# A three-layer graph convolution: the last 148 nodes as an eleventh pair of the seven-product scheme, and all combined operands of the W2 product kept in SBUF

## Chip, cores, metric

One core of one Trainium2 chip. The metric is the device time of one launch in microseconds, median of the runs.

## What is computed

```python
def _gc(x, adj, W, b):
    return adj @ (x @ W) + b
h = jnp.maximum(_layernorm(x, axis=-1), 0.0)
h1 = relu(_gc(h, adj, W1, b1));  h2 = relu(_gc(h1, adj, W2, b2))
out = x + _gc(h2, adj, W3, b3)
```

x is 2708 x 512, adj 2708 x 2708 (dense fp32), W1 512 x 1024, W2 1024 x 1024, W3 1024 x 512. The kernel works on transposed operands (`adjT`, `xT`), with nodes split in two column halves of 1354 (`HALF`), each stored with a stride of 1360.

## The kernel before

**Arithmetic.** Every fp32 operand is cut in two: ScalarE casts it to the matmul's reduced format ("hi"), VectorE subtracts that from the operand ("lo"), and TensorE makes three products (`three`: hi x hi, hi x lo, lo x hi) into one PSUM bank.

**Stages.** Pass 1: adj x LN(x), times 512 features, result `P1` in DRAM. h1 phase: `P1` times W1, in 22 blocks of nodes. Pass 2: adj x h1 for 1024 features. w2 phase: times W2. w3 phase: h2 times W3, again in 22 blocks. Pass 3: adj x (h2 W3), plus b3 and x. Passes and the w2 phase run over three column chunks of 512, 512 and 330 nodes per half (`WIDTH`).

**Seven products.** Pass 2, the w2 phase and pass 3 use a Strassen-like scheme with seven products per chunk: parts `X11, X12, S2, S3, S1, X22, S4` = 0 to 6. A product contracts over ten pairs of 128-node blocks (t, t+10). `DIRECT` parts take raw blocks of adj, the others read combinations that GpSimd made (`TS` in DRAM). Each (chunk, part) is a group on 4 banks in pass 2 and in the w2 phase, on 2 banks in pass 3. Nodes 2560 to 2707 are outside the pairs: block 20 (128 nodes, `left`) with three matmuls per bank, and the 20-node tail (`SHORT`), whose three products are stacked in the rows of one matmul (three loads of 20 rows at `STEP` = 32). They are not in the scheme, so they are added once for every output quarter: in the groups of parts 1, 5 and 6 and in one more with part `None`, which in pass 2 runs inside the group behind (`inner`, `INNER`). `left_over` issues these matmuls (L1811 to L1825).

**Order.** `plan_main` writes one list of steps, which all engines walk in the same order: "cut" (load a raw tile, SyncE; cast, ScalarE; subtract, VectorE), "tail", "drain", "stat", "combine", "store". Raw tiles go through five raw buffers (`RAW`), cut moving tiles through a ring of five (`RING`). `later` places a drain some cuts behind its group. Tiles of h1 or W2 for a later part (`s`, `w2s`) are put between the moving tiles (`spread_in`).

**w2 phase.** Chunk 0's combined operands are made by GpSimd (`prep_moving`, L1618) from `P2` and stored in DRAM (`T2`), from where SyncE loads them (L1023) as raw tiles. For chunks 1 and 2 GpSimd makes them in SBUF (`hold`, `prep_held`, L1641), and they need no raw buffer. Drains of part 0 go to the buffers e(0..3) by ScalarE (L1226), those of the other running sum to e(4..7); finished quarters are stored from these buffers and from `spill` (L1251).

**Start.** `statistics`, `root`, `centre` and `inverse` make the layer norm of each x tile: VectorE and ScalarE take turns.

The change touches `plan_main`, the loads of SyncE, the cuts and drains of ScalarE and VectorE, GpSimd's preparation, and TensorE's group functions.

Of the kernel before, what the change touches and what calls it, by code (L numbers as in the profile page):

```python
# [19 lines left out]
SHORT = 21  # L20
ORDER = (1, 2, 3, 4, 5, 6, 0, 7, 8, 9)
EARLY = 8
BLOCKS = [b for t in ORDER for b in (t, t + PAIRS)] + [20, SHORT]
# [17 lines left out]
HOLD = {S2: 0, S3: 1, S1: 2, X22: 3}  # L41
# [11 lines left out]
INNER = 5  # L53


class Tile:


    def __init__(self, kind, cut):
        self.kind, self.cut = kind, cut  # L60
        self.raw = self.raw_freed = self.slot = None

        self.loads = self.raw_count = None
        self.block = self.part = self.pair = self.chunk = self.half = self.k = None

        self.freed = self.place_freed = None


class Group:


    def __init__(self, phase, chunk, part, banks):
# [3 lines left out]
        self.inner = None  # L76
# [6 lines left out]
class Plan:  # L83
    def __init__(self):
        self.steps, self.groups = [], []
        self.cuts = self.raws = self.slots = self.tails = 0
# [19 lines left out]
    def tile(self, kind, ring, loads=1):  # L106

        j = Tile(kind, self.cuts)
        self.cuts += 1
        if loads:  # L110
            self.take_raw(j, loads)
# [9 lines left out]
    def take_raw(self, j, loads):  # L121
        j.raw = self.raws
        before = self.raw_user[j.raw % RAW]
        j.raw_freed = before.cut + 1 if before else None
# [49 lines left out]

def columns_chunk(block):
    first = block * P
    last = min(first + P, 2 * HALF) - 1
    return max(sum(c % HALF >= a for a in START) - 1 for c in range(first, last + 1))
# [14 lines left out]
def plan_pass1():  # L193
# [31 lines left out]
    for c in range(CHUNKS):  # L225
        mine = []
        for n, b in enumerate(BLOCKS[:-1]):
# [50 lines left out]
def plan_main():  # L278
# [9 lines left out]
    def tail_step(g, c, half):  # L288
        p.tails += 1
        g.tail = (p.tails, c, half, at["tail_freed"][p.tails % 2])  # L290
# [3 lines left out]
    def h1_phase(lag):  # L294
        def emit(g, j):
            def go():
# [3 lines left out]
                if b == SHORT:  # L300
                    p.steps.append(("short", (g, p.drained)))
                    p.later(5, lambda: p.steps.append(("short_stat", (g,))))
                    return
# [4 lines left out]
                if b == 20:  # L308
                    p.stationary("h1", 20, 0, turn, side)
# [8 lines left out]
        for j, b in enumerate(BLOCKS):  # L318
            g = p.group("h1", None, None, [(2 * j) % 8, (2 * j + 1) % 8])
            g.block = b  # L320
            t = p.tile("h1", True, 3 if b == SHORT else 1)
# [4 lines left out]
            p.later(lag if b != SHORT else LAG, emit(g, j))  # L326


    def pass2():
# [10 lines left out]
        leftover = None  # L340
        for part in range(7):
            if part == 0:
                extra = []
            elif part < 6:
                extra = [lambda t=t, i=part + 1: load_h1(i, t) for t in ORDER]
            else:
                extra = [lambda q=q, i=i: load_w2(i, q) for i in (X11, X12, S2) for q in range(4)]
            half = {1: 0, 5: 0, 6: 1}.get(part)
            for c in range(CHUNKS):
# [3 lines left out]
                if leftover:  # L353
                    g.inner = p.group("pass2", leftover.chunk, None, leftover.banks)
                    leftover = None
                for i, t in enumerate(ORDER):
# [3 lines left out]
                    p.release(j, g, half is None and i == PAIRS - 1)  # L360
                    last_of[part, t] = j.freed
                    p.emit_due()
                    if g.inner and i == 0:
                        tail_step(g.inner, g.inner.chunk, 1)
                    if g.inner and i == INNER - 1:
                        k = p.tile("left", True)
                        k.chunk, k.half = g.inner.chunk, 1
                        g.inner.left = k
                        p.release(k, g.inner, True)
                        at["tail_freed"][g.inner.tail[0] % 2] = g.inner.done[-1]  # L370
                        p.later(LAG, lambda q=g.inner: drain2(q))
                        p.emit_due()
                    if half is not None and i == (8 if g.inner else 6):
                        tail_step(g, c, half)
# [3 lines left out]
                if half is not None:  # L378
                    k = p.tile("left", True)
                    k.chunk, k.half = c, half  # L380
                    g.left = k
                    p.release(k, g, True)
                    at["tail_freed"][g.tail[0] % 2] = g.done[-1]
                    p.emit_due()
                last_of["end", part] = g.done[-1]
                p.later(LAG, lambda g=g: drain2(g))
                if part == 4:
                    leftover = g
# [3 lines left out]
    def drain2(g):  # L392
# [3 lines left out]
        if part in (1, 4):  # L396
# [3 lines left out]
            at["staged", c] = bufs  # L400
        elif part is None:
            bufs = at["staged", c]
# [8 lines left out]
        if bufs and part != 4:  # L411
# [9 lines left out]
    def w2_phase():  # L421
# [9 lines left out]
        for c in range(CHUNKS):  # L431
            for part in range(7):
# [6 lines left out]
                if c == 2 and part > 2:  # L439
                    extra = [lambda k=k: load_w3(k) for k in (2 * part - 6, 2 * part - 5)]  # L440
                for q in range(4):
                    held = c > 0 and part in HOLD
# [12 lines left out]
    def drain_w2(g, ms):  # L455
        part = g.part
        spare = [("g", m if g.chunk == 0 else m % 2) for m in ms]
        p.count_drains(g, ms, 2 if part == 4 else 1)
        finals = {1: [("e", 4 + m) for m in ms], 4: spare, 5: [("e", 4 + m) for m in ms],
                  6: [("e", m) for m in ms]}.get(part)  # L460
        needs = {0: [("e", m) for m in ms], 1: [("e", 4 + m) for m in ms], 3: [("e", 4 + m) for m in ms],
# [21 lines left out]
    def w3_phase(lag):  # L483
# [18 lines left out]
        def emit(g, j):  # L502
            def go():
                b = g.block
                if b == SHORT:
                    p.drained += 1
                    g.free_drained = p.drained
                    p.steps.append(("short", (g, p.drained)))
                    p.later(5, lambda: p.steps.append(("short_stat", (g,))))
                    first = late[:2]  # L510
                    del late[:2]
                    for f in first:
                        f()
# [1425 lines left out]
```

## Time and profile before

| | |
|---|---|
| median of three runs | 1592.84 us (1591.72 to 1594.43) |
| the profiled execution | 1593.0 us, span 1591.2 us |
| TensorE matmuls | 7674, busy 1581.1 us (99%) |
| VectorE, ScalarE, GpSimd busy | 872.1, 610.6, 456.3 us |
| DMA | 303.37 MB, mean 191 GB/s |

"Busy" of TensorE is the union of its matmuls, whose ends are modelled and overlap the next one's start. A row of the timeline gives start, length, engine, line, operation, output <- inputs, shapes, and in brackets the idle time before it with what ended it.

### The profile page before, as it was taken

How to read it: one execution, taken by the hardware profiler on the slowest of the kernel's cores; microseconds unless marked ns; L12 is line 12 of the kernel's file. 1: busy time of each engine (PE TensorE's matmuls, PEld its weight loads, DVE VectorE, ACT ScalarE, POOL GpSimd, SP SyncE). 2: the span in 40 equal slices, each digit the busy share in tenths (PEclk: the TensorE clock that was granted, in tenths of full speed). 3: DMA queues.
4: the chain of work that ended last, by engine and by line, in shares of the span. 5: the costliest groups of instructions: out<-in, count | busy, mean ns of one | idle time of the engine just before them, and what ended most of it. 6: DMA issues, size and time to landing. Idle time of an engine off the chain costs nothing.

```text
span 1591.2 us, 20930 instructions
## 1 busy us (share of the span) xinstructions
PE 1581.1 (99%) x7674; PEld 1360.1 (85%) x7674; DVE 872.1 (55%) x1361; ACT 610.6 (38%) x1076; POOL 456.3 (29%) x417
## 2 busy tenths in 40 slices
PE   9999999999999999999999999999999999999999
PEld 7788889988889898989898989788898888888898
DVE  8973433256553443434564446564565538766856
ACT  5442222234433332323332333443455536454444
POOL 5863544336654000000000015345402214201302
PEclk9999999999999999999999999999999999999999
DMA  6975657644567554545455658884645336887866
GB/s 244 321 225 205 222 179 220 204 138 152 176 220 235 151 153 143 142 118 148 143 169 161 175 186 282 275 298 133 206 120 133 93 93 202 251 249 220 252 191 198
DMA packets 196628, 303.37 MB, mean 191 GB/s; under 512 B 22632, under 2 KB 92608, under 8 KB 196524
## 3 DMA queue, kind: packets, MB, share of 16 engines
q1 hardware_dynamic: 162268, 223.12, 47.1%
q0 software_dynamic: 12224, 43.16, 8.4%
q10 hardware_dynamic: 22032, 35.74, 6.3%
q8 instruction: 61, 1.00, 0.3%
q14 instruction: 43, 0.35, 0.1%
HBM read 219.44 MB, written 82.50 MB: 190 GB/s over the span
## 4 chain that ended last, share of the span: by engine, by line
PE 91%; DVE 5%; DMA 3%; ACT 1%; issue 0%; ACTq 0%; DVEq 0%
PE ps L1731 30%; PE ps L1733 30%; PE ps L1732 30%; DVE slots L1350 1%; PE ps L1824 1%; DVE still L1332 1%; DMA H<-parts 1%; DVE stats L1279 1%; DMA raw<-adjT 0%; DMA raw<-W 0%; DVE ring L1360 0%; DMA raw<-TS 0%; DMA P<-stage_b 0%; DMA raw<-T 0%; ACT slots L1099 0%
## 5 line engine op out<-in xcount | busy, mean ns | idle before, releaser
L1360 DVE TENSOR_TENSOR ring<-raw,ring 128x512 fp32r<-128x512 f32 (+1 forms) x562 | 404.7, 732 | 426.6 <-ACT ring L1131 424.1
L1131 ACT CAST ring<-raw 128x512 fp32r<-128x512 f32 (+1 forms) x562 | 321.3, 577 | 561.9 <-PE ps L1733 464.8
L1731 PE MATMUL ps<-slots,still 128*128 128x512 f32 (+1 forms) x504 | 183.6, 364 | 2.3 <-DVE slots L1350 1.4
L1733 PE MATMUL ps<-slots,still 128*128 128x512 f32 (+1 forms) x504 | 183.1, 363 | 0.0
L1732 PE MATMUL ps<-slots,still 128*128 128x512 f32 (+1 forms) x504 | 183.1, 363 | 0.0
L1733 PE MATMUL ps<-ring,even 128*128 128x512 f32 (+1 forms) x480 | 174.6, 364 | 0.0
L1732 PE MATMUL ps<-ring,even 128*128 128x512 f32 (+1 forms) x480 | 174.6, 364 | 0.0
L1731 PE MATMUL ps<-ring,even 128*128 128x512 f32 (+1 forms) x480 | 174.6, 364 | 0.0
L1587 POOL DMA_DIRECT2D prep<-P x40 | 26.4, 662 | 465.2 <-DMA P<-U 434.4
L1731 PE MATMUL ps<-ring,S 128*128 128x512 f32 (+1 forms) x420 | 153.0, 364 | 0.6 <-DVE ring L1360 0.6
L1733 PE MATMUL ps<-ring,S 128*128 128x512 f32 (+1 forms) x420 | 152.5, 363 | 0.0
L1732 PE MATMUL ps<-ring,S 128*128 128x512 f32 (+1 forms) x420 | 152.5, 363 | 0.0
L1350 DVE TENSOR_TENSOR slots<-raw,slots 128x1024 fp32r<-128x1024 f32 (+2 forms) x64 | 86.3, 1348 | 118.5 <-ACT slots L1099 118.4
L1733 PE MATMUL ps<-ring,odd 128*128 128x512 f32 (+1 forms) x360 | 131.1, 364 | 0.0
L1732 PE MATMUL ps<-ring,odd 128*128 128x512 f32 (+1 forms) x360 | 131.1, 364 | 0.0
L1731 PE MATMUL ps<-ring,odd 128*128 128x512 f32 (+1 forms) x360 | 131.0, 364 | 0.0
L1731 PE MATMUL ps<-ring,W2c 128*128 128x512 f32 (+1 forms) x336 | 122.8, 365 | 2.6 <-ACT parts L1226 1.5
L1732 PE MATMUL ps<-ring,W2c 128*128 128x512 f32 (+1 forms) x336 | 122.5, 365 | 0.0
L1733 PE MATMUL ps<-ring,W2c 128*128 128x512 f32 (+1 forms) x336 | 122.5, 365 | 0.0
L1099 ACT CAST slots<-raw 128x1024 fp32r<-128x1024 f32 (+2 forms) x64 | 59.7, 933 | 142.8 <-PE ps L1733 134.2
L1731 PEld LDWEIGHTS ps<-slots,still 128*128 128x128 f32 x504 | 94.8, 188 | 18.3 <-DVE slots L1350 3.8
L1733 PEld LDWEIGHTS ps<-slots,still 128*128 128x128 f32 x504 | 94.8, 188 | 13.2
(162 smaller groups left out, 2891.1 us busy)
## 6 DMA issues: line engine op xcount, KB each, us to landing
raw<-TS SPq DMA_DIRECT2D x160, 256.0 KB, 2.9
raw<-adjT SPq DMA_DIRECT2D x138, 256.0 KB, 3.1
raw<-adjT SPq DMA_DIRECT2D x41, 512.0 KB, 4.6
TS<-made SPq DMA_DIRECT2D x20, 1024.0 KB, 6.6
raw<-TS SPq DMA_DIRECT2D x80, 165.0 KB, 2.4
raw<-HS SPq DMA_DIRECT2D x50, 256.0 KB, 2.7
raw<-P SPq DMA_DIRECT2D x45, 256.0 KB, 4.0
raw<-adjT SPq DMA_DIRECT2D x68, 165.0 KB, 2.6
```

What stands on the lines that cost most here:

```text
L1099: act.copy(slot1(j, 0, a, j.chunk), raw1[:, j.raw % RAW1, a, 0:w]) \
L1131: act.copy(hi, src).then_inc(hi_done, 1)
L1279: dve.bn_stats(stats[rows, half:half + 6], tile).then_inc(stats_done, 1)
L1332: dve.scalar_tensor_tensor(still[:, j.block, 1, :], xin[:, j.block, 1, :], x_column(n, "scale"), still[:, j.block, 0, :].bitcast(F32), ALU ...
L1350: dve.tensor_tensor(slot1(j, 1, a, j.chunk), raw1[:, j.raw % RAW1, a, 0:w], slot1(j, 0, a, j.chunk).bitcast(F32), ALU.subtract).then_inc(l ...
L1360: dve.tensor_tensor(lo, src, hi.bitcast(F32), ALU.subtract).then_inc(lo_done, 1)
L1587: pool.dma_start(dst, src).then_inc(prep_in[i], 16)
L1731: pe.matmul(out, st_hi, mv_hi, start=start, stop=False)
L1732: pe.matmul(out, st_hi, mv_lo, start=False, stop=False)
L1733: return pe.matmul(out, st_lo, mv_hi, start=False, stop=stop)
L1824: pe.matmul(ps[:, g.banks[m], 0:w], tail[0:REP, cols], slot_tails[g.tail[0] % 2][0:REP, 0:w], start=False, stop=True).then_inc(group_done, 1)
```

## The change

The 148 last nodes become an eleventh pair (`EXTRA`) of two blocks of 74 nodes (`REST`), with all seven products. So every group of pass 2 and pass 3 (21 each) ends with `extra_pair`: per bank two matmuls over 128 rows that hold the three stacked products: rows 0 to 73 of the first lo x hi, rows 74 to 127 of it and 74 to 127 of the second hi x hi, rows 0 to 73 of the second hi x lo. `AGAIN` (54) rows and the other `ONCE` (20) are loaded a second time for that. The part `None` and `inner` are gone. The stationary combinations of the extra pair go through DRAM (`HX`, `HX3`) and come back as tiles `extra2` (two per part) and `extra3` (one per group of pass 3, four transfers); the combined rows of adj come from `TX`, which GpSimd makes after the h1 phase. In the w2 phase `hold` serves chunk 0 as well: S2, S3 are made beside pass 2, S1, X22 once pass 2 is over and U is stored; the places in `HOLD` are reversed, and `T2` is gone. `sides` swaps e(0..3) and e(4..7) from chunk to chunk. The blocks of the h1 and w3 phases run with the extra pair in the ninth place. At the start, `root(1)`, `centre(1)` and `inverse(1)` move behind the cut of the first tile's second half. In pass 3 the part-4 group finishes three quarters (before: two in part `None`, one in part 4).

```diff
+REST = 74
+EXTRA = PAIRS
+BLOCKS = [b for t in ORDER[:EARLY] + (EXTRA,) + ORDER[EARLY:] for b in ((20, 21) if t == EXTRA else (t, t + PAIRS))]
+AGAIN = P - REST
+ONCE = REST - AGAIN
-HOLD = {S2: 0, S3: 1, S1: 2, X22: 3}
+HOLD = {S2: 3, S3: 2, S1: 1, X22: 0}
...
+def sides(chunk):
+    return (0, 4) if chunk % 2 == 0 else (4, 0)
...
+        def load_extra(part):
+            first = p.tile("extra2", False, 2)
+            second = p.tile("extra2", False, 2, low=False)
+            for row, j in enumerate((first, second)):
+                j.part, j.half = part, row
+                j.place_freed = ("group", last_of["end", part - 2]) if part > 1 else None
...
-                extra = []
+                extra = [lambda i=i: load_extra(i) for i in (X11, X12)]
             elif part < 6:
-                extra = [lambda t=t, i=part + 1: load_h1(i, t) for t in ORDER]
+                extra = [lambda i=part + 1: load_extra(i)] + [lambda t=t, i=part + 1: load_h1(i, t) for t in ORDER]
...
-                    if n % 3 == 1 if part < 6 else n > 3 and n % 2 == 0:
+                    if n % 5 in (1, 3) if part < 6 else n > 3 and n % 2 == 0:
                         spread_in(extra)
...
-                    held = c > 0 and part in HOLD
+                    held = part in HOLD
...
-            for part in (0, 1, 2, 3, None, 4, 5, 6):
+            for part in range(7):
...
+                    if i == 2:
+                        k = p.tile("extra3", False, 4)
+                        n = 7 * c + part
+                        k.part, k.pair = part, n % 3
+                        k.place_freed = ("group", ends[n - 3] if n > 2 else w3_end)
...
-    left = place("left", [P, 2, H], F32R, left_at)
+    extra_at += -extra_at % BANK
+    extra2 = place("extra2", [P, 2, 2, F], F32R, extra_at)
...
                 elif j.kind == "left":
-                    sp.dma_start(raw[:, r, 0:WIDTH[j.chunk]], adjT[20 * P:21 * P, columns(j.half, j.chunk)]) \
-                        .then_inc(raw_in[r], 16)
+                    w = WIDTH[j.chunk]
+                    sp.dma_start(raw[0:REST, r, 0:w], extra_rows(j.part, j.chunk, 0, REST)).then_inc(raw_in[r], 16)
+                    sp.dma_start(raw[REST:P, r, 0:w], extra_rows(j.part, j.chunk, 0, AGAIN)).then_inc(raw_in[r], 16)
+                elif j.kind == "extra2":
...
+                    sp.dma_start(raw[0:REST, r, :], src).then_inc(raw_in[r], 16)
+                    sp.dma_start(raw[REST:P, r, :], src[again, :]).then_inc(raw_in[r], 16)
+                elif j.kind == "extra3":
...
+                    for half in range(2):
+                        cols = slice(half * QUARTER, (half + 1) * QUARTER)
+                        again = slice(0, AGAIN) if half == 0 else slice(ONCE, REST)
+                        sp.dma_start(raw[0:REST, r, cols], src).then_inc(raw_in[r], 16)
+                        sp.dma_start(raw[REST:P, r, cols], src[again, :]).then_inc(raw_in[r], 16)
...
-                    for r in range(3):
-                        sp.dma_start(raw_tail[r * STEP:r * STEP + TAIL, 0, 0:WIDTH[c]],
-                                     adjT[SHORT * P:N, columns(half, c)]).then_inc(tail_in, 16)
+                    sp.dma_start(raw_tail[0:REST, 0, 0:w], extra_rows(a.part, c, 0, REST)).then_inc(tail_in, 16)
+                    sp.dma_start(raw_tail[REST + AGAIN - ONCE:P, 0, 0:w], extra_rows(a.part, c, AGAIN, REST)) \
+                        .then_inc(tail_in, 16)
...
                 for second in (False, True):
+                    if second and c == 0:
+                        pool.wait_ge(group_done, at["pass2_end"])
+                        for u in range(CHUNKS):
+                            pool.wait_ge(u_stored[u], 16 * KF)
...
+            def extra_pair(g, ms, first, second):
...
+                    pe.matmul(out, first[:, cols], ring[:, j.slot % RING, 0, 0:w], start=False, stop=False)
+                    pe.matmul(out, second[:, cols], slot_tails[g.tail[0] % 2][:, 0:w], start=False, stop=True) \
+                        .then_inc(group_done, 1)
```

## Rows read from the trace of the kernel before

**Rows 1.** The page: span, TensorE's busy time, its granted clock in 40 slices.
```profile
span 1591.2 us, 20930 instructions
...
PE 1581.1 (99%) x7674; PEld 1360.1 (85%) x7674; DVE 872.1 (55%) x1361; ACT 610.6 (38%) x1076; POOL 456.3 (29%) x417
...
PEclk9999999999999999999999999999999999999999
```

**Rows 2.** Stages: us, busy (x count) of PE, PEld, DVE, ACT, POOL, clock, DMA share, GB/s.
```profile
0.00:76.00 76.00, 72.80 (x299) 56.63 (x300) 69.69 (x155) 38.52 (x66) 51.03 (x35) 1.00 0.80 277
...
439.00:987.00 548.00, 548.00 (x2713) 476.50 (x2712) 255.13 (x395) 170.88 (x309) 59.73 (x70) 1.00 0.57 173
987.00:1141.00 154.00, 152.89 (x675) 126.17 (x674) 92.20 (x131) 65.18 (x108) 68.37 (x72) 1.00 0.69 225
...
1314.00:1519.00 205.00, 205.00 (x907) 169.80 (x906) 149.24 (x205) 103.40 (x179) 48.23 (x42) 1.00 0.78 233
1519.00:1591.00 72.00, 68.48 (x451) 67.37 (x449) 46.95 (x92) 33.95 (x76) 11.39 (x14) 1.00 0.70 201
```

**Rows 3.** Timeline of TensorE in pass 2, first matmul of and behind two blocks.
```profile
538.78 0.40 PE L1731 MATMUL ps<-ring,left 128*128 128x512 f32 x1
...
542.51 0.39 PE L1731 MATMUL ps<-ring,odd 128*128 128x512 f32 x1
...
591.87 0.32 PE L1731 MATMUL ps<-ring,left 128*128 128x330 f32 x1
...
594.34 0.40 PE L1731 MATMUL ps<-ring,even 128*128 128x512 f32 x1
```

**Rows 4.** The same in pass 3, one wide block.
```profile
1340.94 0.39 PE L1731 MATMUL ps<-ring,left 128*128 128x512 f32 x1
...
1342.76 0.39 PE L1731 MATMUL ps<-ring,S 128*128 128x512 f32 x1
```

**Rows 5.** Timeline of TensorE: four stands, at the start, in w2, in pass 3.
```profile
10.94 0.50 PE L1731 MATMUL ps<-slots,still 128*128 128x512 f32 x1 [0.89 <-DVE slots L1350]
...
1032.12 0.50 PE L1731 MATMUL ps<-ring,W2c 128*128 128x512 f32 x1 [1.11 <-DVE ring L1360]
...
1157.17 0.39 PE L1731 MATMUL ps<-ring,W2c 128*128 128x330 f32 x1 [1.52 <-ACT parts L1226]
...
1550.27 0.42 PE L1731 MATMUL ps<-ring,S 128*128 128x330 f32 x1 [0.56 <-DVE ring L1360]
```

**Rows 6.** Timeline of ScalarE before the stand at 1032.
```profile
1028.52 0.62 ACT L1131 CAST W2c<-raw 128x512 fp32r<-128x512 f32 x1 [2.32 <-DMA raw<-W]
```

**Rows 7.** Timeline of VectorE, cut of the first tile's second half.
```profile
10.19 0.69 DVE L1350 TENSOR_TENSOR slots<-raw,slots 128x512 fp32r<-128x512 f32 x1 [0.21 <-ACT slots L1099]
```

**Rows 8.** Timeline of ScalarE's and GpSimd's queues: U stores, and loads that begin steps.
```profile
997.06 1.35 ACTq L1243 DMA_DIRECT2D P<-U  x3
...
1020.03 1.29 POOL L1587 DMA_DIRECT2D prep<-P  x2 [10.97 <-DMA H<-parts]
...
1031.71 1.28 POOL L1587 DMA_DIRECT2D prep<-P  x2 [0.30 <-POOL hold L1670]
...
1060.64 0.72 POOL L1587 DMA_DIRECT2D prep<-P  x1 [0.30 <-POOL hold L1670]
...
1068.98 1.28 POOL L1587 DMA_DIRECT2D prep<-P  x2 [0.31 <-POOL hold L1664]
```

**Rows 9.** Timeline of ScalarE at the end of the h1 phase: relu, then casts.
```profile
434.66 1.06 ACT L1175 ACTIVATE pair_buf<-pair_buf 128x1024 f32<-128x1024 f32 x1 [2.84 <-DVE pair_buf L1402]
...
436.71 1.65 ACT L1131 CAST ring<-raw 128x512 fp32r<-128x512 f32 x3
```

**Rows 10.** The DMA view: packets; issues with KB each and median us to landing.
```profile
DMA packets 196628, 303.37 MB, mean 191 GB/s; under 512 B 22632, under 2 KB 92608, under 8 KB 196524
...
P<-U ACTq DMA_DIRECT2D x4, 165.0 KB, 4.5
...
raw_tail<-adjT SPq DMA_DIRECT2D x48, 40.0 KB
```

More of the change, by code:

```diff
@@ L104, in later, with tile @@
         self.pending.sort(key=lambda q: q[0])
-    def tile(self, kind, ring, loads=1):
+    def tile(self, kind, ring, loads=1, low=True):
         j = Tile(kind, self.cuts)
         self.cuts += 1
+        if low:
+            self.lows += 1
+            j.low = self.lows
         if loads:
@@ L504, in go @@
                 b = g.block
[L505 to L513, printed above, removed]
-                    return
-                if b == 20:
-                    buf = ("stash", 4)
-                elif b % PAIRS >= EARLY:
+                if EARLY <= pair_of(b) < PAIRS:
                     buf = ("stash", 2 * (b % PAIRS - EARLY) + b // PAIRS)
@@ L616, in store @@
                 p.steps.append(("store", (g, finals, number)))
-            p.later(4 if part == 1 else 2, store)
+            p.later({1: 4, 4: 9}.get(part, 2), store)
     h1_phase(2)
@@ L948, in _, with wait_h1, extra_rows @@
             seen = {"p1": 0, "h2": -1}
+            def wait_h1():
+                seen["h1"] = 1
+                for i in range(PAIR_BUFS):
+                    sp.wait_ge(kept_stored[i], kept(i, PAIRS + 1))
+                    sp.wait_ge(sums_stored[i], sums(i))
+            def extra_rows(part, c, first, last):
+                if part in DIRECT:
+                    k, a = DIRECT[part]
+                    start = 2 * PAIRS * P + k * REST
+                    return adjT[start + first:start + last, columns(a, c)]
+                i = {S2: 3, S3: 1, S1: 0, X22: 2}[part]
+                if ("tx", c) not in seen:
+                    seen["tx", c] = 1
+                    for k in (0, 2):
+                        sp.wait_ge(prep_out[k], 16 * (c + 1))
+                return TX[i, first:last, within(c)]
             def load(j):
@@ L1117, in cut @@
                     act.wait_ge(group_done, 8 * CHUNKS)
+                if j.kind == "extra2" and j.part == X11:
+                    act.wait_ge(made_done, 4 * made_total)
+                    act.wait_ge(lo1_done, len(tiles1))
+                if j.kind == "extra3":
+                    act.wait_ge(g_stored[0], plan.stored["g", 0])
                 if j.kind == "w2s" and j.part == S2:
@@ L1790, in block_group @@
                 if g is w3_groups[0]:
-                    pe.wait_ge(lo_done, max(j.cut for k, j in steps if k == "cut" and j.kind == "w3w") + 1)
+                    pe.wait_ge(lo_done, max(j.low for k, j in steps if k == "cut" and j.kind == "w3w"))
                 halves = range(2) if g.phase == "h1" else (0,)
+                rows = block_width(g.block)
                 for n, j in enumerate(g.tiles):
-                    pe.wait_ge(lo_done, j.cut + 1)
+                    pe.wait_ge(lo_done, j.low)
                     s = j.slot % RING
@@ L1799, in block_group @@
                         for q in range(KF):
-                            hi, lo = (ring[:, s, i, q * P:(q + 1) * P] for i in range(2))
+                            hi, lo = (ring[:, s, i, q * P:q * P + rows] for i in range(2))
                             if g.phase == "h1":
@@ L1804, in block_group @@
                                 mv = [W3c[:, n * KF + q, i, :] for i in range(2)]
-                            mm = three(ps[:, g.banks[half], :], hi, lo, mv[0], mv[1], start=n == 0 and q == 0,
+                            mm = three(ps[0:rows, g.banks[half], :], hi, lo, mv[0], mv[1], start=n == 0 and q == 0,
                                        stop=n == len(g.tiles) - 1 and q == KF - 1)
```

499 lines of the change are left out of this document (244 added, 255 removed).

## Prediction

> **What bounds the kernel now.** I read the page first. TensorE is busy for 1581.1 of 1591.2 us at full granted clock in all 40 slices [rows 1]; the other engines are far below. The stage table says the same stage by stage: in the product with the adjacency behind the first layer (439 to 987 us, "pass 2" below) TensorE is busy 548.00 of 548 us, in the product with W2 (987 to 1194) it loses 1.1 us before 1141, and in the last product (1314 on, "pass 3") it is full until 1519 and loses 3.5 us behind it, the drain of the end included [rows 2]. So two things can move the time: the number and length of matmuls, and new waits. The matmul rows must be read by their starts: a 512-wide one is drawn 0.39 us long, but the next starts after 0.23.
>
> **Fewer matmuls.** Nodes 2560 to 2707 now cost, per 512-node column half and chunk, a block of three matmuls (`ring`, `left`) and one for the 20-row tail, on 4 banks in pass 2. The trace has 12 such blocks there; a wide one takes 542.51 - 538.78 = 3.73 us (16 matmuls, 0.233 each), a narrow one 594.34 - 591.87 = 2.47 us (0.154 each) [rows 3]. Eight wide and four narrow: 39.7 us. The change takes the 148 nodes as an eleventh pair of 74 + 74 rows: 7 products in place of 8, each packed into two matmuls (222 rows in 2 x 128). That is 21 groups x 4 banks x 2 = 168 matmuls, 112 wide and 56 narrow. At 0.2275 us, the pitch of the same kind in pass 3 [rows 4] (the new operand lies on a 512-byte border, as all others that run at this pitch, where `left` did not), it is 25.5 + 8.6 = 34.1 us; at 0.233 it is 34.7. Saved: 5.6 us (5.0 the other way). Pass 3 has 12 blocks of 8: 1342.76 - 1340.94 = 1.82 us wide [rows 4], 1.23 narrow by 0.154, together 19.5 us; it becomes 56 x 0.2275 + 28 x 0.154 = 17.0 us. Saved 2.5. In all 8.0 us (7.4 to 8.2). The groups with 74 rows in the first-layer and W3 phases keep their number (24 + 24 matmuls each side) and their 512 moving columns; I give them nothing. No row has 74 stationary columns; the nearest, the 128-column ones, price them at par, and the bound is 96 x 0.02 = 2 us either way.
>
> **Waits that go.** (1) In chunk 0 of the W2 product every combined operand comes as a DMA of its own (`raw<-T`) between those of the weights, through five raw buffers. At 1032.12 TensorE had stood 1.11 us for a cut whose ScalarE had waited for `raw<-W` [rows 5, 6]; start to start that is 1.11 + 0.39 - 0.23 = 1.3 us. The change takes 16 of these loads away: the operands are made in `hold`, so the weight loads run far ahead. (2) At 1157.17 it stood 1.52 us (1.7 start to start) for a copy into `e(m)`, whose last store of the chunk before had not landed [rows 5]. `sides` swaps the two halves of the buffers from chunk to chunk, so the copy meets buffers stored one part (7 us) earlier. Together -3.0 us; if another wait takes their place, 0.
>
> **What the new order costs.** (3) At the start `root(1)`, `centre(1)` and `inverse(1)` move behind the cut of the second half of the first tile. The stand of 0.89 us at 10.94 goes [rows 5], but VectorE cuts first and then does the four small operations for the next x tile, which it did before 10.19 while ScalarE worked [rows 7]: the x chain comes about 0.3 us later, and VectorE, busy 69.7 of the first 76 us [rows 2], is what the later stands of this stage wait for. I take +0.3 (from -1.0 to +0.5). (4) GpSimd must make S2, S3 of chunk 0 beside pass 2, and S1, X22 only when pass 2 is over and U is stored. One step took 1068.98 - 1060.64 = 8.3 us in chunk 1 [rows 8]. The last U stores were issued from 997.06, 0.45 us each, so the fourth by 998.9, and land in 4.5 us [rows 8, 10]: 1003.4. The last S1 follows after three steps and 5.5 us of a fourth, at 1033.8, and is cut by 1035. TensorE reaches it at 987 + 19 x 2.73 = 1039. These 4 us of cover are gone if a step takes 9.7 us, and at 11.7, the longest (1020.03 to 1031.71, [rows 8]), the stand is 6 us. Taken 0. (5) At the seam to pass 2, the last groups' relu (1.06 us, [rows 9]), their cast, two casts of the extra operand and one of the third moving tile, 4 x 0.55 [rows 9], the drain before and VectorE's last cut, 0.7 each [rows 7], end 5 to 5.4 us after the last first-layer group, and TensorE has two tiles, 5.4 us, in hand: +0.2 (0 to 1.5). (6) Later parts of pass 2 wait on ScalarE for the end of a group before the extra operand can be cut; that delays the third tile to 2.4 us behind it, against 5.4 in hand: 0. (7) Pass 3 gets per group one `extra3`, one `left`, one tail. VectorE gains per group a tail and a 256-wide cut, 0.7 and 0.4 by the 0.69 of the 512-wide one [rows 7], and was busy 149 of 205 us and 47 of 72 [rows 2], 21 such pairs are 23 us; SyncE issues 18 DMAs per group, 8.1 of 9.9 us in the narrow chunk by the 0.45 of [rows 8]. There it stood 0.56 us at 1550.27 already [rows 5]. I take +0.5 there (0 to 6, the latter one such stand in each narrow group).
>
> Sum: -8.0 - 3.0 + 0.3 + 0.2 + 0.5 = -10.0 us. Against the profiled execution, 1593.0 us (span 1591.2), 1583.0; the median of the runs is 1592.84, so **1582.8 us**. The likeliest case's own range is 1578 to 1588.
>
> **Rival on the other side: two DMA engines become the bound in pass 3 (slower).** All raw loads of before have 128 rows but the tail's, 20. How were these split? The page's 22632 packets under 512 B [rows 10] are 4608 pieces of 80 B (9 loads of 20 columns), 256 for the two bias tables, and 17768 closing packets. The DMA view lists 1142 transfers, 84 of them with 20 rows: 1142 x 16 - 84 x 6 = 17768. So 128 rows went to 16 engines, and 20 rows to 10, two each. That fits equal shares (the largest divisor up to 16) and shares rounded up alike. For 74 rows they part: equal shares mean 2 engines with 37 rows, rounded up means 15 with 5. Should it be 2, and always the same 2, one wide group of pass 3 gives each of them 37 rows of `left` and of the tail at 2 KB and of both halves of `extra3` at 1 KB (222 KB), 28 KB of the 54- and 20-row pieces, 160 KB of ten moving tiles and 37 KB of results and x (16 transfers of 16 KB a chunk): 447 KB. One engine moved 277/(16 x 0.80) = 21.6 GB/s in the first stage and 233/(16 x 0.78) = 18.7 in pass 3 [rows 2], so a group takes 21.2 to 24.5 us against 64 x 0.2275 = 14.6 for TensorE. Narrow: 319 KB, 15.1 to 17.5 against 9.9. 14 x 6.6 + 7 x 5.2 = 129 us, or 192: **1712 to 1775 us**. Rounded up, or spread over changing engines, a wide group is about 255 KB, 14 us at most, and stays hidden. It decides from some 290 KB per engine and wide group on. In pass 2 it is 441 KB in 29 us, 21 to 24 us, and 172 KB more in one group of three, whose excess the next one takes: little is lost there, 0 to 3 us. For it: both sizes seen are equal shares. Against it: two sizes prove no rule, nothing shows that the engines are the same each time.
>
> The Trainium skill speaks for this rival: "DMA: Bandwidth & Descriptors", section "Why a DMA increments its semaphore by 16 and not by 1", says that the number of engines is the largest up to 16 that divides both sides' slowest dimension, and on the hardware queues the lowest-numbered ones. The trace's 10 engines for 20 rows agree, its choice of engines no row shows; by that rule the time is the rival's.
>
> **Rival: a wait takes the place of the two removed.** GpSimd late with S1 by 6 us, (4), gives 1588.8; the narrow chunk of pass 3 at +6 gives 1588.3; both 1594.3, the only way of this kind over the line. For it: a step of 11.7 us is in the trace [rows 8]; against it: that one was made beside the 16 `T` loads and their stores, which are gone.
>
> **Rival: it doesn't save what it says.** If 74-column groups ran longer or the packed pairs had to wait for the tail each time (21 waits of 0.4 us), the 8 us are eaten: 1591.
>
> **How the numbers follow.** Forecast 0.54; DMA engines 0.38; a wait in place 0.05; no saving 0.03. A measurement of this kernel tells 0.2%, 3.2 us, from no change: faster is below 1589.6. The forecast and half of the two small rivals are faster, 0.56; same 0.05; slower 0.39. The rival with 0.38 must be in the range for 8 in 10: its lower two thirds, up to 1750. Low end 1578, from the small bounds in (3) and the matmul term.
>
> **What would show it.** Right: 7638 matmuls (36 fewer), TensorE busy 99%, blocks with `extra2` of 8 matmuls in 1.82 us, no gap at about 1025 and 1150, no `raw<-T`, pass 3 of 275 us. Rival: pass 3 of 400 us or more, TensorE there below 7 tenths, waiting for ring cuts behind `raw` loads, and landings of `raw<-adjT` over 6 us. I'd be wrong too if pass 2 grew, or if the seam at 439 us showed more than 1.5 us.

## The result, and the profile after

The changed kernel takes 1762.17 us (median of four runs, 1756.61 to 1767.89) against 1592.8: the ratio is 1.1063, 95% interval 1.1023 to 1.1102, so it is 169 us slower. The time lies inside what the prediction had worked out for its DMA rival, 1712 to 1775 us, and outside the stated range, whose upper end was 1750. Of the profiled execution (1767.9 us, span 1766.1) the page says:

```profile
span 1766.1 us, 21256 instructions
...
PE 1632.7 (92%) x7638; PEld 1380.9 (78%) x7638; DVE 852.0 (48%) x1360; ACT 641.5 (36%) x1145; POOL 503.3 (28%) x454
...
PE   9999999999898989999999999989998787877876
...
PEclk9999999999999999999999999999999988898988
...
PE 58%; DMA 21%; DVE 7%; POOL 5%; SPq 3%; issue 2%; ACT 2%; ACTq 1%; POOLq 0%; DVEq 0%
```

[rows 1] had TensorE at 99%, now it is at 92%, with 7638 matmuls, the 36 fewer that were forecast. The row of the granted clock dips in the last eight slices, and the last line, the chain of work that ended last, has 21% of DMA in it. The same by stages (columns as in [rows 2]; the borders have moved by up to 26 us):

```profile
0.00:77.00 77.00, 72.90 (x302) 57.24 (x303) 70.34 (x159) 39.86 (x68) 52.32 (x36) 1.00 0.82 281
77.00:440.00 363.00, 363.00 (x1769) 311.91 (x1768) 171.60 (x217) 113.02 (x155) 185.55 (x145) 1.00 0.59 188
440.00:1006.00 566.00, 547.37 (x2690) 474.45 (x2690) 251.72 (x386) 190.46 (x344) 100.91 (x100) 0.98 0.61 187
1006.00:1340.00 334.00, 326.36 (x1539) 276.83 (x1538) 175.69 (x297) 145.81 (x289) 112.28 (x119) 0.98 0.52 153
1340.00:1626.00 286.00, 224.27 (x845) 170.52 (x843) 127.56 (x193) 106.60 (x187) 37.45 (x38) 0.90 0.59 178
1626.00:1764.00 138.00, 98.79 (x502) 89.93 (x500) 55.09 (x111) 45.72 (x103) 14.78 (x18) 0.88 0.53 156
```

In the last product (the two last rows) TensorE is busy 78% and 72% of the time, while the DMA engines' mean share is only 0.59 and 0.53, less than the 0.78 and 0.70 of before: a mean over 16 engines says nothing of two of them. Stage by stage, from the first matmul of one to the first of the next (us):

| | pass 1 | h1 phase | pass 2 | W2 and W3 | last product |
|---|---|---|---|---|---|
| before | 312.4 | 119.7 | 548.1 | 326.5 | 274.0 |
| changed | 313.5 | 119.7 | 565.8 | 333.9 | 422.6 |

Of the 175 us between the two profiled executions (1767.9 and 1593.0), 148.6 are in the last product, 17.7 in pass 2 and 7.4 in the W2 product. Worked out from the starts of the first matmul behind each group, a wide group of the last product takes 17.3 to 25.0 us, 21.8 in the mean of the 13 behind the first, where its 64 matmuls need 14.5; a narrow one 14.2 to 19.3, 16.5 in the mean, for 9.8. The rival had 21.2 to 24.5 and 15.1 to 17.5. Its sign "TensorE below 7 tenths" did not come (0.78 and 0.72), since matmuls behind a stand run at a lower clock and so count as busy for longer; its others did. Single landings in pass 2 took 12 us as well, by the chain of the changed kernel:

```profile
524.86 12.12 DMA raw<-adjT
...
609.70 11.93 DMA raw<-TS
```

Three stands by TensorE's timeline (in brackets the stand and what ended it), at the head of pass 2, in the narrow chunk of the W2 product and in the first group of the last product, with the matmuls behind the last:

```profile
459.91 0.77 PE L1811 MATMUL ps<-ring,even 128*128 128x512 f32 x1 [7.04 <-DVE ring L1446]
...
1188.01 0.61 PE L1811 MATMUL ps<-ring,W2c 128*128 128x330 f32 x1 [7.64 <-DVE parts L1562]
...
1349.89 0.77 PE L1811 MATMUL ps<-ring,S 128*128 128x512 f32 x1 [5.72 <-DVE ring L1446]
...
1353.87 0.63 PE L1811 MATMUL ps<-ring,S 128*128 128x512 f32 x1
1354.30 0.51 PE L1812 MATMUL ps<-ring,S 128*128 128x512 f32 x1
1354.64 0.39 PE L1813 MATMUL ps<-ring,S 128*128 128x512 f32 x1
1354.87 0.40 PE L1811 MATMUL ps<-ring,S 128*128 128x512 f32 x1
```

And the longest pieces of the chain that ended last, from 1400 us on: landings of `extra3`'s loads, 9 us each for 74 KB or less:

```profile
1401.27 8.90 DMA raw<-HX
1489.78 9.01 DMA raw<-HX
1510.91 9.12 DMA raw<-HX
1531.03 8.68 DMA raw<-HX
```

### The profile page after: what moved, and what is told of

It reads as the page before. It is cut to its first block, busy times and chain, and to the rows that moved or that the text cites. A ratio compares the mean times of both kernels' runs of the same rounds, so it can differ in the third digit from the quotient of the medians.

```text
span 1766.1 us, 21256 instructions
## 1 busy us (share of the span) xinstructions
PE 1632.7 (92%) x7638; PEld 1380.9 (78%) x7638; DVE 852.0 (48%) x1360; ACT 641.5 (36%) x1145; POOL 503.3 (28%) x454
## 4 chain that ended last, share of the span: by engine, by line
PE 58%; DMA 21%; DVE 7%; POOL 5%; SPq 3%; issue 2%; ACT 2%; ACTq 1%; POOLq 0%; DVEq 0%
PE ps L1811 19%; PE ps L1812 19%; PE ps L1813 19%; DMA raw<-HX 7%; DMA prep<-P 6%; DMA raw<-adjT 3%; DMA raw<-TS 2%; DMA prep<-xT 2%; DVE ring L1446 2%; SPq L1058 2%; POOL parts L1806 2%; ACT ring L1195 1%; SPq L1057 1%; DVE slots L1428 1%; DMA HX<-pair 1%
## 5 line engine op out<-in xcount | busy, mean ns | idle before, releaser
L1446 DVE TENSOR_TENSOR ring<-raw,ring 128x512 fp32r<-128x512 f32 (+1 forms) x522 | 369.1, 726 | 464.8 <-ACT ring L1195 462.4
L1195 ACT CAST ring<-raw 128x512 fp32r<-128x512 f32 (+2 forms) x564 | 316.4, 573 | 513.4 <-PE ps L1813 272.7
L1811 PE MATMUL ps<-ring,S 128*128 128x512 f32 (+1 forms) x420 | 174.4, 415 | 99.2 <-DVE ring L1446 96.2
L1811 PEld LDWEIGHTS ps<-ring,S 128*128 128x128 f32 x420 | 89.0, 212 | 133.2 <-DVE ring L1446 78.7
L1813 PE MATMUL ps<-ring,even 128*128 128x512 f32 (+1 forms) x480 | 175.6, 366 | 0.0
L1813 PE MATMUL ps<-ring,S 128*128 128x512 f32 (+1 forms) x420 | 167.4, 399 | 0.0
L1812 PE MATMUL ps<-ring,S 128*128 128x512 f32 (+1 forms) x420 | 167.3, 398 | 0.0
L1660 POOL DMA_DIRECT2D prep<-P x48 | 30.9, 645 | 356.3 <-DMA P<-U 348.9
L1806 POOL TENSOR_TENSOR parts<-parts,prep 128x512 f32<-128x512 f32 (+1 forms) x24 | 31.5, 1329 | 320.6 <-DVE parts L1572 167.5
L1811 PEld LDWEIGHTS ps<-ring,even 128*128 128x128 f32 x480 | 91.3, 190 | 27.3 <-issue 9.1
```

Of the source, the lines that this page charges most:

```text
L1195: act.copy(hi, src).then_inc(hi_done, 1)
L1446: dve.tensor_tensor(lo, src, hi.bitcast(F32), ALU.subtract).then_inc(lo_done, 1)
L1660: pool.dma_start(dst, src).then_inc(prep_in[i], 16)
L1806: pool.tensor_tensor(tile, tile, prep[:, i, 0:WIDTH[c]], ALU.add).then_inc(finished, 1)
L1811: pe.matmul(out, st_hi, mv_hi, start=start, stop=False)
L1812: pe.matmul(out, st_hi, mv_lo, start=False, stop=False)
```

## Experiments

**Which engines carry 74 rows.** The theory is the rival's: a 74-row transfer is shared by two DMA engines, always the same. Its own rival: what costs is the number of small transfers. e1 cuts every 74-row load by SyncE in two, e2 only those of the last product, e3 the same ones as e2 at another row (the diff in short):

```diff
-sp.dma_start(raw[0:REST, ...], src).then_inc(raw_in[r], 16)
+for a, b in ((0, cut), (cut, REST)):      # e1, e2: cut = 64; e3: cut = 37
+    sp.dma_start(raw[a:b, ...], src[a:b]).then_inc(raw_in[r], 16)
```

> The changed kernel, with every load of 74 rows by SyncE (the moving tile of the extra pair, its tail, extra2, extra3) issued as two, 64 rows and 10 rows; the same bytes to the same places. Theory (a 74-row transfer is shared by 2 DMA engines, always the same, a 64-row one by 16): the last product falls from 422.6 us to 273 to 282, the product behind the first layer from 565.8 to 545 to 550, TensorE's stand of 7.8 us at 1180 us, which waits for GpSimd, stays within 3 us of that; the whole is 1590 to 1603 us. Rival (what costs is the number of small transfers, or reading the rows twice): 7 more issues per group make it no faster, 1760 us or more.

> The same 64 + 10 split in the last product alone. Theory: the last product 273 to 282 us, the product behind the first layer as in the changed kernel, 563 to 568, so the whole is about 1762 - 145 = 1617 us (1612 to 1625). Rival (number of transfers): 1760 or more.

> As e2, but the 74-row loads of the last product are issued as 37 + 37 rows: the same number of transfers and the same bytes as in e2. Theory (equal shares on the lowest engines; 37 is a prime, so each half goes to one engine, the same one): that engine gets 444 + 28 + 160 + 37 = 669 KB in a wide group and 490 KB in a narrow one, at 21 GB/s 31.9 and 23.3 us, the last product takes about 610 us and the whole 1950 (1900 to 2030). Rival one (number of transfers): as e2. Rival two (few engines, but another set each time, or shares rounded up): as e2, within 10 us.

Measured: e1 1639.21 us (ratio to before 1.0300, 1.0268 to 1.0332), last product 321.6, pass 2 546.7. e2 1655.66, last product 319.4, pass 2 564.2. e3 1922.34, last product 582.4, its wide groups 27.8 to 33.9 (30.5 in the mean), its narrow ones 22.9 (31.9 and 23.3 were expected, and 1900 to 2030 for the whole). e2 and e3 issue the same number of transfers with the same bytes; only the row at which they are cut differs, and 263 us lie between their last products. That excludes the number of transfers, and "another set each time" as well. The packet lines of four pages count the engines. The changed kernel:

```profile
DMA packets 211554, 319.55 MB, mean 181 GB/s; under 512 B 28262, under 2 KB 103904, under 8 KB 211450
```

e1:

```profile
DMA packets 214915, 319.57 MB, mean 196 GB/s; under 512 B 31622, under 2 KB 107264, under 8 KB 214810
```

e2:

```profile
DMA packets 213571, 319.57 MB, mean 193 GB/s; under 512 B 30278, under 2 KB 105920, under 8 KB 213466
```

e3:

```profile
DMA packets 211555, 319.56 MB, mean 166 GB/s; under 512 B 28262, under 2 KB 103904, under 8 KB 211450
```

The counts fit one small closing packet for each engine that takes part. e1 has 140 transfers more than the changed kernel and 3360 small packets more, 24 each: 16 (64 rows) + 10 (10 rows) - 2 (74 rows). e2: 84 more and 2016, again 24. e3: 84 more and none: 1 + 1 - 2, a 37-row transfer has one engine. The Trainium skill, "DMA: Bandwidth & Descriptors", section "Why a DMA increments its semaphore by 16 and not by 1", states this rule, the largest k up to 16 that divides both sides' slowest dimension, and that on the hardware queues these are the lowest-numbered engines. The packet counts agree with the rule, and the times of e3 with its transfers meeting on the same engine; the engines' numbers no run here shows.

e1 and e2 missed their own numbers, though: 1590 to 1603 and 1612 to 1625 us were expected for the whole, 273 to 282 for the last product of both. Pass 2 of e1 came out; its last product kept 47.6 us more than before. The stand in the product with W2, which was expected to stay, shrank from 7.64 to 1.45 us (e8 below tells what makes it). The stage rows of e1, last product in its wide and narrow part:

```profile
1309.00:1531.00 222.00, 203.27 (x855) 163.27 (x855) 130.54 (x200) 110.74 (x193) 41.63 (x42) 0.97 0.80 239
1531.00:1632.00 101.00, 86.82 (x493) 80.43 (x491) 52.02 (x104) 45.54 (x98) 11.01 (x14) 0.94 0.68 193
```

By groups: most wide ones are at 14.5, the first takes 20.5, that of part 6 24.3 and 24.2 us, and six of the seven narrow ones 11.6 to 15.2 instead of 9.8. So a second cause sits under the first.

**Two small parts undone.** e4 is e1 with

```diff
-    extra_at += -extra_at % BANK
-    return (0, 4) if chunk % 2 == 0 else (4, 0)
+    return (0, 4)
```

> e1 with two small parts of the change undone: extra2 starts off the 512-byte border again (64 bytes on), and the two halves of the drain buffers are no longer swapped from chunk to chunk in the W2 product. Theory: the 112 wide matmuls with extra2 start 0.233 us apart instead of 0.227 (0.7 us in all), and a stand of 1 to 2 us behind ScalarE's or VectorE's drain appears where the narrow chunk of the W2 product begins, unless the GpSimd stand there covers it; the whole within 4 us of e1. Rival (the pitch of 0.233 came from the block of three matmuls and not from the place): pitch 0.227 as before the undoing.

Measured 1650.95 us. The block of eight matmuls with `extra2`, first matmul of it and first behind it, in the changed kernel and in e4:

```profile
478.06 0.39 PE L1901 MATMUL ps<-ring,extra 128*128 128x512 f32 x1
...
479.88 0.39 PE L1811 MATMUL ps<-ring,even 128*128 128x512 f32 x1
```

```profile
476.21 0.40 PE L1909 MATMUL ps<-ring,extra 128*128 128x512 f32 x1
...
478.08 0.39 PE L1819 MATMUL ps<-ring,even 128*128 128x512 f32 x1
```

1.82 us against 1.87, so 0.2275 and 0.234 each: the place of the operand does it, as forecast. The expectation calls the place of e4 "64 bytes on"; by the kernel's addresses it is 320 bytes past a multiple of 512 (64 past one of 256), counted from the start of its memory, and which of these borders counts no run shows. In the narrow chunk of the W2 product TensorE stood 0.54 and 0.59 us at 1163 and 1171 without the swap, and 1.45 at 1161 with it (e1): no gain from the swap. The whole is 12 us over e1, not within the 4 expected: 4.8 of it are in pass 1, where both have the same code, and 6.0 in pass 2, with a stand of 2.12 us at 534 that neither edit explains. Single executions differ by that much, so of e4 only the pitch and the stands are used.

**What is left in the last product.** In e1 ScalarE's timeline shows the stand in the group of part 6, the second behind part 4 (the expectation of e5 calls it "the group behind part 4"):

```profile
1404.97 0.62 ACT L1204 CAST ring<-raw 128x512 fp32r<-128x512 f32 x1 [0.21 <-DMA raw<-adjT]
1411.80 0.82 ACTq L1352 DMA_DIRECT2D outT<-parts  x2
1412.72 0.62 ACT L1204 CAST ring<-raw 128x512 fp32r<-128x512 f32 x1 [7.12 <-POOL parts L1815]
```

ScalarE issues, some tiles later, the store of a quarter that part 4 finishes, and waits for GpSimd's addition of x to it; GpSimd does this quarter as the third of three, with 4 to 6 us of loading x before each of the last two. All ring casts are queued behind. e5 turns GpSimd's order round, e6 brings `extra3` with one transfer instead of six, e7 loads `extra2` later, e8 takes one wait of GpSimd in the W2 product behind its load. e5 is made from e1, and each of the others contains the ones before it.

```diff
 # e5
-4: [(2, 0, 1, 5), (0, 1, 0, 6), (6, 1, 1, 4)]
+4: [(6, 1, 1, 4), (2, 0, 1, 5), (0, 1, 0, 6)]
 # e6: HX3 of shape (7, 128, 512), stored in the form of the tile
+sp.dma_start(raw[:, r, :], HX3[EXTRA_PLACE[j.part], :, :]).then_inc(raw_in[r], 16)
 # e7
-extra = [lambda i=i: load_extra(i) for i in (X11, X12)]
+extra = [lambda: None, lambda: None, lambda: load_extra(X11), lambda: None, lambda: load_extra(X12)]
 # e8, in prep_held
-if second and c == 0:                # ahead of the loads of the second half
+if second and c == 0 and q == 0:     # behind the first two of them
     pool.wait_ge(group_done, at["pass2_end"])
```

> e1 with the three finishes of part 4 of the last product in another order: GpSimd adds x to the quarter that ScalarE stores first, and to the two that VectorE needs a group later behind it. Theory (in e1 ScalarE stands 7.1 us for the third finish, its casts behind it): the group behind part 4 falls from 24.3 and 24.2 us in the wide chunks to 14.5 to 16, the last product from 321.6 to about 302 us, the whole from 1639 to about 1618 (1613 to 1625). Rival (GpSimd is late in any order, and VectorE's drain of part 5 stands for it then): these groups stay at 19 us or more.

> e5 with the operand extra3 stored in DRAM in the form of its tile, so that one load of 128 rows brings it in place of six (64, 10 and 54 rows, twice). Same bytes; a group of the last product has 17 loads in place of 22. Theory (SyncE's issues, 0.35 to 0.5 us each, bound the narrow groups): narrow groups fall from 11.6 to 14.7 us to 9.8 to 11, the last product by 10 to 18 us against e5. Rival (the bytes bound them, or the five raw buffers): they stay above 11.5. It may cost up to 3 us before the last product, since ScalarE and GpSimd issue 24 stores in place of 4.

> e6 with the tiles of extra2 for parts 0 and 1 loaded behind the seventh moving tile of the first group of pass 2 and in the group behind it, not behind the second and fourth. Theory (in e1 these loads and casts stand ahead of the moving tiles while VectorE is still busy with the first-layer drains; TensorE stood 1.4 and 2.6 us and then ran 9 matmuls at the lower clock): the first group loses at most 1.5 us, the product behind the first layer takes 541 to 543 us in place of 546.7. Rival (the seam is set by the drains of the first layer alone): 546 or more.

> e7 with the wait for the end of pass 2 and for U's stores, ahead of GpSimd's second half of chunk 0, moved behind the first loads of that half. Theory: GpSimd's chain of 20 steps starts 4 to 5 us earlier against the end of pass 2, and the last step of the narrow chunk too; TensorE's stand at the head of the narrow chunk of the W2 product, which in e1 waits for a drain and not for GpSimd, stays at 1 to 2 us; the product with W2 within 1 us of e7. The whole 1590 to 1600 us if e5, e6 and e7 come out by their theories.

| | whole | pass 2 | W2 and W3 | last product | group of part 6, wide | seven narrow groups |
|---|---|---|---|---|---|---|
| e1 | 1639.2 | 546.7 | 324.1 | 321.6 | 24.3, 24.2 | 89.3 |
| e5 | 1630.8 | 546.7 | 324.8 | 312.7 | 17.6, 17.9 | 91.5 |
| e6 | 1616.4 | 548.4 | 331.3 | 292.4 | 15.6, 16.8 | 83.3 |
| e7 | 1611.5 | 544.2 | 329.2 | 291.3 | 16.8, 16.3 | 82.4 |
| e8 | 1603.1 | 543.8 | 322.9 | 293.7 | 16.5, 16.3 | 84.1 |

(e1 and e8 are medians, the others one execution each; the stages are of the profiled one. Single executions of like code differ: by 6 us in pass 1, 2 us in the last product of e1 and e2. So only the stage that an edit touches is compared.) e5: the order was worth 6.5 us at each of two places, 8.9 in the stage where 20 were expected; the two groups came down, yet not to 14.5 to 16. e6: 20.3 us less, more than the 10 to 18 expected; but the narrow groups took only 8 of them and stayed at 9.7 to 14.6, so the number of SyncE's issues is part of the answer there, about 8 of some 20 us. Before the last product its stores cost 0.5 us in the W3 phase (120.2 for 119.7); the rest of the 6.5 us there is a stand of 5.46 us at 1167 in the W2 product, where e5 and e6 have the same code. e7: pass 2 at 544.2 against the 541 to 543 expected; the stand of 2.57 us is gone, one of 1.03 stays. e8 (1603.14 us, ratio 1.0078, 1.0048 to 1.0109) came out above its 1590 to 1600. Its W2 product is 6.3 us shorter than e7's, where no more than 1 had been expected, and e9 to e12, which keep this edit, repeat it: 322.4 to 322.9 us for W2 and W3 in all five, and no stand, where all eight changed kernels without the edit have one. This tells who made the stand in the narrow chunk. It is ended by a drain in name (e7),

```profile
1164.23 0.39 PE L1818 MATMUL ps<-ring,W2c 128*128 128x330 f32 x1 [4.54 <-DVE parts L1571]
```

but e8 changes only when GpSimd's chain starts. The drain stood behind a cast of ScalarE, and this behind GpSimd's last `hold` tile; in the changed kernel the chain runs

```profile
1184.71 0.88 POOL hold L1744
...
1185.70 0.63 ACT W3c L1195
...
1186.96 0.91 DVE parts L1562 x2
...
1188.01 0.61 PE ps L1811
```

Counted from the first matmul of the W2 product, GpSimd's last step ends after 179.6 us in the changed kernel (stand 7.64), 177.1 in e6 (5.46), 176.2 in e7 (4.54), 175.6 in e2 (3.92), 173.9 in e5 (2.20) and 173.1 in e1 (1.45; e4, without the swap, stands twice): each stand is that time less 171.7 to 171.9 us. In e8 to e12 it ends after 163.8 to 164.5. Its twenty steps differ by some us from one execution to the next with the same code (153.3 us in e5, 156.6 in e6), by their loads. My e8 expectation, "waits for a drain and not for GpSimd", was wrong.

**Tails, and the swap again.** e9 lets GpSimd issue the tails of the narrow chunk, e10 is e8 without `sides`, e11 puts the tail behind the sixth tile:

```diff
 # e9, in GpSimd's loop over the steps of the last product
+if kind == "tail" and a.phase == "pass3" and a.chunk == 2: (the three tail loads)
 # e10
-    return (0, 4) if chunk % 2 == 0 else (4, 0)
+    return (0, 4)
 # e11, in pass3
-                    if i == 0:
+                    if i == 5:
                         tail_step(g, c)
```

> e8 with the three loads of the tail in the narrow chunk of the last product issued by GpSimd, which is idle there, in place of SyncE. Theory (in e8 SyncE's 17 issues and their waits for raw buffers take 10.9 to 14.4 us per narrow group): narrow groups 9.8 to 12, the last product 285 to 290 us in place of 293.7, the whole 1594 to 1600 against 1603. Rival (the landing of loads and the five raw buffers bound them, not the issuing): groups as in e8, the whole within 2 us of it.

> e8 without the swap of the two halves of the drain buffers from chunk to chunk in the W2 product. In e8 the stand of 1.5 to 1.7 us at the head of the narrow chunk, which the kernel before has too, is gone. Theory (the swap took it away): without it 1 to 2 us of stands appear there again, ended by ScalarE's or VectorE's drain. Rival (e8's earlier GpSimd took it away, the swap does nothing): none over 0.3 us.

> e8 with the three loads of the tail behind the sixth moving tile of each group of the last product, not behind the first, so that they don't stand right behind the three loads of the extra pair's moving tile. Theory (six small loads close together, 3 us of SyncE in which only one moving tile is sent for, starve the five raw buffers): narrow groups fall from 10.9 to 14.4 us (84.1 for the seven) to 9.8 to 12 (under 77), the last product from 293.7 to 286 or less. Rival (the extra landings and buffers as such): the sum of the narrow groups stays within 3 us of 84.

e9: 1607.18 us (ratio 1.0103, 1.0085 to 1.0120), no faster than e8 (1594 to 1600 expected), and its last product takes 294.5 us against e8's 293.7. Its first six narrow groups took 65.5 us against e8's 70.6, but the last one 20.2 against 13.5, since its tail loads stood behind GpSimd's additions of x (issued from 1586.05 us):

```profile
1588.97 0.47 ACT L1249 CAST slot_tail<-raw_tail 128x330 fp32r<-128x330 f32 x1 [8.37 <-DMA raw_tail<-adjT]
```

e10: 1602.96 us, W2 and W3 322.9 as in e8, no stand in the narrow chunk: the swap does nothing here that can be seen. e11: the narrow groups sum to 77.9 (under 77 expected), the last product to 286.7 (286 or less), so 7.0 us less than e8 in that stage and nearly the theory, if by one execution (e6, e7, e8 and e10 lie at 291.3 to 293.8). The whole, 1604.66, doesn't show it: pass 1 and pass 2 of that execution were 5.7 and 3.2 us longer with the same code.

**Half of the change.** e12 keeps e8 up to the product with W2, and the kernel before from the W3 phase on.

> e8 up to the product with W2 (the eleventh pair in the product behind the first layer with its 74-row loads split, the combined operands in SBUF), and the kernel before from the W3 phase on: there the 148 nodes are outside the pairs again, with block 20 in 128 rows and the 20-row tail. So the change without its part in the last product. Theory (of the forecast's saving the terms before the last product are real, 5.6 and 3 us, and the last product costs what it did): 543 us for the product behind the first layer, 322 to 324 for those with W2 and W3, 274 for the last, the whole 1585 us (1580 to 1590), faster than the kernel before by 3 to 13. Rival (the gain of e8 in the first stages is noise of the chip, or the last product suffers from them): 1590 or more.

1588.09 us over 12 runs against 1592.29 over 17 of before: ratio 0.9975, 0.9961 to 0.9989. The profiled execution took 1584.0 us. Pass 2, W2 with W3, and the last product:

```profile
438.00:982.50 544.50, 541.85 (x2689) 470.60 (x2688) 256.00 (x386) 189.72 (x344) 103.10 (x103) 1.00 0.64 194
982.50:1305.00 322.50, 322.50 (x1539) 275.72 (x1538) 179.12 (x295) 145.15 (x287) 106.35 (x111) 1.00 0.53 160
1305.00:1580.00 275.00, 274.21 (x1357) 238.50 (x1355) 196.47 (x297) 137.24 (x254) 59.47 (x56) 1.00 0.75 225
```

No stand in the second row, 2.7 us in the first. The stages are within 2 us of the expected ones (544.7, 322.4 and 274.0 from first matmul to first matmul). It is 4 us faster than the kernel before (by the interval 2 to 6) and 174 faster than the changed one, and the only kernel of this study that beats both.

## Why the prediction was wrong, step by step

**The step that failed** is the choice between the forecast and its DMA rival. The sum took the loads of the last product as hidden ("about 255 KB, 14 us at most, and stays hidden") and gave the stage +0.5 us. The runs showed 422.6 us in place of 274.0: with the 74-row loads cut into 64 and 10 it is 321.6, so 101 us of it came from their two engines, and 47.6 us stay above before that neither forecast nor rival had. The rival's mechanism was right, and so were its prices for a group: 21.2 to 24.5 us a wide one (21.8 measured in the mean, 17.3 to 25.0 singly), 15.1 to 17.5 a narrow one (16.5). That its whole, 1712 to 1775, holds the measured 1762 is in part luck: by the measured means of the groups its way of adding gives 1583 + 14 x 7.2 + 7 x 6.6 = 1730, and it had 0 to 3 us for pass 2, which lost 18, and nothing for the W2 product, which lost 7. I gave it 0.38 because two sizes of transfer prove no rule and no row showed that the engines are the same each time. Both doubts were fair for the trace alone, but nothing stood against the rule either: both sizes seen were equal shares, and the trace held no row for "rounded up". The Trainium skill, "DMA: Bandwidth & Descriptors", section "Why a DMA increments its semaphore by 16 and not by 1", states the rule that gives the rival. And once it has 0.38, cutting off its upper third to save width put the end of the range at 1750 and the time outside it. Two smaller slips changed nothing: the forecast and half of the two small rivals are 0.58, not 0.56, and in (4) a step of 11.7 us, over three steps and two thirds, gives 8 us of stand, not 6.

**The terms of the sum**, one by one:

- Fewer matmuls, -8.0 us: the count and the pitch are right, 7638 matmuls and `extra2` blocks of 1.82 us, and e4 showed that the pitch comes from the operand's place. In time, pass 2 of e7 to e12 took 541.9 to 547.0 us, 544.1 in the mean, against 548.1: -4.0 where -5.6 + 0.2 was forecast. The 2.5 us of the last product no run shows, since with seven groups a chunk it never came below 286.7.
- Waits that go, -3.0: right in size (326.5 to 322.4 in e12 is -4.1), half wrong in cause. The first, for `raw<-T`, goes. The second I put down to a store of e(m) [rows 5] and gave to `sides`; e10 has neither the swap nor the stand, so the swap isn't what took it away. What did was not tried part by part.
- The start, +0.3: the stand at 10.94 us became one of 0.52 at 13.33. But pass 1 came out between 310.2 and 316.4 us in kernels with the same code there, so the term can't be measured.
- GpSimd's hold for chunk 0, 0: true of chunk 0, and the wrong place to look. Its chain of twenty steps runs from 1019.85 to 1185.6 us with no pause over 0.7 between two steps, and the twentieth, not the fourth, was late: the stand of 7.64 us, in the narrow chunk. Four steps more had been put ahead of chunks 1 and 2 (sixteen steps end 160.3 us behind the first matmul of the W2 product in the kernel before), and I followed the queue only to its first consumer.
- The seam to pass 2, +0.2 (0 to 1.5): 1.26 and 7.04 us in the changed kernel, 1.41 and 2.57 in e1, 1.03 in e7. Left out were the eight transfers of `extra2` (twelve in e1) that SyncE sends between the first moving tiles.
- The last product, +0.5 (0 to 6): mis-sized most. With the 64 + 10 cut the stage took 321.6 us in e1, 50 above the 271.5 that the sum has without this term. e5 takes 8.9 of them (ScalarE behind GpSimd's third finish; I had counted VectorE's and SyncE's work and not the store that ScalarE issues), e6 another 20.3 (six small loads for one tile), e11 7.0 (small loads side by side). The remaining 15 us (286.7 in e11) are open.
- The rival's "little is lost" in pass 2, 0 to 3 us: 19.1, by e1. The excess of one group was not taken by the next: at the head and early in parts 1 and 2, where loads of `extra2` and of h1 tiles stand between the moving ones, TensorE stood 7.04, 5.26 and 5.07 us, and started six to nine matmuls behind each 0.427 us apart in place of 0.227.

So the 175 us between the profiled executions are, by their differences: from the changed kernel to e1, 101 us of two-engine transfers in the last product (422.6 to 321.6) and 19 in pass 2, 10 in the stages of W2 and W3 and 2 in pass 1; and from before to e1, 48 us in the last product that the cut of the transfers doesn't take away, less 5 that e1 saves in the stages ahead of it. The 10 us are not shown to come from two engines: e2, with the changed kernel's code up to the last product, has 328.6 us there against 333.9.

## What to carry to other kernels

Before a tile gets a number of rows that 16 doesn't divide, work out how many DMA engines its transfers will have: here 74 rows went over two, and cutting them into 64 and 10 gave back 123 us. A mean DMA share of 0.59 doesn't exclude a DMA bound, nor does a tile's byte count: the groups took the time of the bytes on the engine that had most (by the prediction's estimate 447 KB, in 21.8 us). Where a stage is moved to another engine's queue, follow that queue to its last step, and list what every engine issues, stores too, in the narrowest group.

## What the hardware showed that was not expected

A crowded DMA engine holds up the issuing queue itself. SyncE issues 457 loads and stores in the last product of e2 and as many in e3; one took over 1.5 us to issue in e2, and 101 in e3. In e1 two of SyncE's split loads are issued in 1.0 us; in e3, where the two halves go by one engine, the same two take 3.4 to 5.4, and tiles queued behind them for other engines go out that much later (SyncE's timeline of e3):

```profile
1500.42 3.37 SPq L990 DMA_DIRECT2D raw_tail<-adjT  x2
1503.84 2.27 SPq L1105 DMA_DIRECT2D raw_tail<-adjT  x1
1506.15 1.26 SPq L1033 DMA_DIRECT2D raw<-adjT  x2
1507.46 5.37 SPq L990 DMA_DIRECT2D raw<-HX  x2
```

And a stand costs more than its length: behind the 5.72 us at 1349.89 nine matmuls in a row started 0.427 us apart, the lower of the two clock levels, 1.2 GHz, before they returned to 0.227 and the upper, 2.4 GHz; with the ones at both ends that is 2.3 us on top. The granted clock (third figure from the end) of these matmuls and of those behind them, in the changed kernel:

```profile
1349.90:1354.10 4.20, 4.20 (x10) 3.33 (x11) 4.09 (x9) 3.05 (x7) 2.04 (x1) 0.50 0.80 220
1355.00:1357.00 2.00, 2.00 (x11) 1.63 (x10) 0.81 (x1) 0.62 (x1) 1.84 (x3) 1.00 0.85 263
```

It was 0.90 in the wide part of the last product and 0.88 in the narrow, and 0.79 and 0.71 in e3, where the stands are longer; in the kernel before it was 1.00.
